# One level of Strassen's algorithm for the neighbour product A times g in a two-layer graph network kernel

## The reference

```python
h = jnp.maximum(_layernorm(x, axis=-1), 0.0)
x = x + _L0_gnn_ref(h, edge_weight, L0_gnn_bias, edge_index)     # h @ W.T + bias, W summed from the edges
h = jnp.maximum(_layernorm(x, axis=-1), 0.0)
x = x + _L1_gnn_ref(h, src, dst, W_self0, W_neigh0, b0, W_self1, W_neigh1, b1)
...
def _sage_layer(h, edge_src, edge_dst, deg_inv, W_self, W_neigh, b):
    agg = jax.ops.segment_sum(h[edge_src], edge_dst, num_segments=h.shape[0])
    return h @ W_self + (agg * deg_inv[:, None]) @ W_neigh + b
h = relu(_sage_layer(x, ..., W_self0, W_neigh0, b0)); out = _sage_layer(h, ..., W_self1, W_neigh1, b1)
```

## Time and profile before

| | before |
|---|---|
| time, median of 3 runs | 805.08 us (804.27 to 805.58) |
| span of the profiled execution | 802.3 us |
| time of the profiled execution outside its span | not shown; 2.8 us if it ran as the median |
| PE busy | 769.9 us (96%) |
| DVE busy | 485.3 us (60%) |
| ACT busy | 370.8 us (46%) |
| POOL busy | 412.3 us (51%) |
| DMA moved | 151.40 MB |

### The profile page before, as it was taken

The page is one execution under the profiler, slowest core; times in us unless marked ns, Lnnn a source line. Parts: engine busy times, 40 slices in busy tenths (PEclk is TensorE's granted clock), DMA queues, the critical chain, the costliest instruction groups (busy, mean ns, idle before and its releaser), DMA issues.

```text
span 802.3 us, 13275 instructions
## 1 busy us (share of the span) xinstructions
PE 769.9 (96%) x4553; PEld 639.1 (80%) x4554; DVE 485.3 (60%) x720; ACT 370.8 (46%) x526; POOL 412.3 (51%) x569
## 2 busy tenths in 40 slices
PE   3878999999999999999999999999999999999998
PEld 2767888888888888888887888888888888887787
DVE  7989377777554788867413342136568766246444
ACT  7757634333364232223246886453233223347653
POOL 5000167676649899765742210127899756724311
PEclk9689999999999999999999999999999999999999
DMA  3112456775565853577855654566745659667654
GB/s 111 42 57 92 137 178 192 237 228 186 191 225 193 275 169 116 182 230 269 278 180 189 210 158 105 171 209 229 261 134 164 202 198 332 216 206 268 223 163 142
DMA packets 83239, 151.40 MB, mean 189 GB/s; under 512 B 10979, under 2 KB 21278, under 8 KB 83168
## 3 DMA queue, kind: packets, MB, share of 16 engines
q1 hardware_dynamic: 61646, 102.65, 40.8%
q10 hardware_dynamic: 20002, 42.91, 15.0%
q0 software_dynamic: 1520, 4.92, 1.5%
HBM read 103.79 MB, written 46.65 MB: 188 GB/s over the span
## 4 chain that ended last, share of the span: by engine, by line
PE 82%; DVE 8%; DMA 3%; POOL 3%; issue 2%; ACT 2%; POOLq 0%; SPq 0%; ACTq 0%; DVEq 0%
PE bank L1449 45%; PE bank L1493 18%; PE bank L1384 13%; DVE L L1676 2%; DVE R L1661 2%; PE bank L1280 1%; PE bank L1296 1%; DVE L L1668 1%; PE bank L1510 1%; DMA cst<-prod1g_scratch 1%; DMA b<-in_L_gnn_b 1%; PE bank L1377 1%; PE bank L1275 1%; POOL split L935 1%; ACT Ax L1160 1%
## 5 line engine op out<-in xcount | busy, mean ns | idle before, releaser
L1449 PE MATMUL bank<-slot,split 128*128 128x512 f32 x1680 | 386.3, 390 | 0.2 <-POOL split L935 0.2
L1449 PEld LDWEIGHTS bank<-slot,split 128*128 128x128 f32 x1680 | 313.7, 188 | 66.0 <-issue 1.5
L897 POOL TENSOR_TENSOR AT<-AT,az 128x50 int32 (+3 forms) x288 | 95.5, 332 | 119.7 <-DMA az<-asum_scratch 78.7
L935 POOL TENSOR_TENSOR split<-stage,split 128x512 fp32r<-128x512 f32 x50 | 66.5, 1331 | 116.9 <-ACT split L1128 116.8
L1160 ACT CAST Ax<-AT 128x1280 fp32r<-128x1280 uint16 x40 | 106.6, 2667 | 34.5 <-PE bank L1493 27.5
L1811 DVE TENSOR_TENSOR slot<-T,slot 128x512 fp32r<-128x512 f32 x64 | 90.1, 1430 | 23.8 <-ACT slot L1119 22.0
L1384 PE MATMUL bank<-slot,split_m 128*128 128x512 f32 x320 | 91.2, 396 | 0.0
L1933 DVE SCALAR_TENSOR_TENSOR cst<-bank,dinv,stage 128x512 f32<-128x512 f32 (+1 forms) x41 | 30.3, 738 | 94.8 <-PE bank L1493 94.6
L1128 ACT CAST split<-stage 128x512 fp32r<-128x512 f32 x50 | 31.1, 624 | 118.1 <-PE bank L1449 67.4
L1493 PE MATMUL bank<-slot,Ax 128*128 128x512 f32 (+1 forms) x336 | 77.6, 383 | 0.4 <-ACT Ax L1160 0.4
L952 POOL TENSOR_TENSOR T<-T,wst 128x512 f32<-128x512 f32 x48 | 69.4, 1462 | 5.2 <-DMA wst<-in_L_gnn_W_self 5.2
(11 more groups left out here) (193 smaller groups left out, 1030.6 us busy)
## 6 DMA issues: line engine op xcount, KB each, us to landing
stage<-hT_scratch SPq DMA_DIRECT2D x90, 256.0 KB, 3.6
wst<-in_L_gnn_W_neigh SPq DMA_DIRECT2D x56, 256.0 KB, 4.3
wst<-in_L_gnn_W_self SPq DMA_DIRECT2D x56, 256.0 KB, 3.3
x1b_scratch<-x ACTq DMA_DIRECT2D x10, 512.0 KB, 6.1
hT_scratch<-hTs ACTq DMA_DIRECT2D x10, 512.0 KB, 3.2
stage<-prod0s_scratch SPq DMA_DIRECT2D x20, 256.0 KB, 3.0
hT_scratch<-h1s ACTq DMA_DIRECT2D x20, 256.0 KB, 3.5
stage<-prod1s_scratch SPq DMA_DIRECT2D x20, 256.0 KB, 2.7
```

The lines of the kernel that those rows point to most:

```text
L897: pool.tensor_tensor(a, a, az32[:, n % NZ, pairs * pos:pairs * (pos + 1)], ALU.add) \
L935: pool.tensor_tensor(split[:, v % 2, 1, :], source(v), split[:, v % 2, 0, :].bitcast(F32), ALU.subtract).then_inc(s_olo, 1)
L1449: last = pe.matmul(dense_bank(v, which)[:, :], split[:, v % 2, a, NT * k:NT * (k + 1)], slot[t % 2][:, b, HF * (HK * which + k):HF * (HK * ...
```

## The change

A times g is now also done with one level of Strassen's algorithm. A's rows and g's rows are halves of five tiles, g's columns halves of 512, so a layer has seven products of five row tiles, 35 steps u, each of 5 source tiles times 2 parts, 10 matmuls. The order of the steps is `A_SEQ`.

- **A turned once.** ACT copies the 16-bit counts of each of the ten row tiles from stride ten to contiguous (`turn`), at the product steps v = 10 to 19 of layer 0. Tile 0 goes to `az`, the others into `AT`.
- **Left operands.** Ring `Ax` of three, each 128x640. Where the quarter of A stands alone (p = 0, 1, 4) ACT widens it. Where it is a sum (p = 3, 2, 6, 5) DVE makes it (`left_sum`).
- **Right operands.** g12 and g21 are no longer stored to DRAM. DVE forms T1 and T2 (`first_sums`, at the last five product steps), T4 (`fourth_sum`) and T3 (`third_sum`); ACT rounds all seven (`right_hi`), POOL makes the rests (`right_lo`) except those of B21, which DVE makes (`b21_lo`).
- **Gathering.** ACT copies the first product out (`keep_first_A`); DVE adds products 3 and 2 (`take`), adds the kept sum times dinv into the sums tile (`sums_ready`), and takes the 20 outputs. Outputs come at u = 2, 4, 6, 8, 9, 17, 19, 21, 23 to 34. In layer 1 POOL adds x1 for 15 of the 20 tiles (`add_x1`), DVE for 5. Four sums tiles and four result tiles instead of two.
- **Bias.** It is added in `sub_products` at p = 0, p = 1 (once) and p = 2 instead of in `finish_tile`.
- **Stores.** Outputs of layer 1 are issued by ACT instead of POOL; the last tile is no longer split.
- **First weight blocks of layer 1.** ACT rounds them at u = 25 to 32, POOL instead of DVE makes the rest (`first_block_lo`).
- The heavier form is taken from a degree over 2048.

```diff
+A_SEQ = by_pairs(0, 1) + [(3, i) for i in range(PAIRS)] + by_pairs(2, 6) + by_pairs(5, 4)
+WIDENED = {0: (0, 0), 1: (0, 1), 4: (1, 1)}
+RIGHT_A = {0: "B11", 1: "B21", 2: "T1", 3: "T2", 4: "T4", 5: "T3", 6: "B22"}
...
+            def turn(n):
+                act.wait_ge(s_degs, n + 1)
+                ...
+                act.copy(turned(n).rearrange("p (s d) -> p s d", s=TN),
+                         ATd[:, NT * n:NT * (n + 1), :].rearrange("p d s -> p s d")).then_inc(s_turn, 1)
...
+            def neighbours(layer, u, heavy):
+                ...
+                wait_operand(pe, layer, u)
+                for k in range(PAIRS):
+                    if i == 0:
+                        wait_low(pe, layer, RIGHT_A[p], k)
+                    for b, part in enumerate(right(layer, RIGHT_A[p], k)):
+                        last = pe.matmul(sums, Ax[:, u % NR_A, NT * k:NT * (k + 1)], part, ...)
...
                 if p == 0:
+                    dve.tensor_tensor(q[:, 0, 1, i, :], dense_bank(v, 1)[:, :], b0[:, 0:HF], ALU.add).then_inc(s_evb, 1)
                     return
...
-                    elif p == 2:
-                        last = dve.tensor_tensor(second, first, ps, ALU.add)
+                    elif p == 2:
+                        link(dve.tensor_tensor(second, first, ps, ALU.add))
+                        last = dve.tensor_tensor(second, second, b0[:, HF:F], ALU.add)
...
+            def left_sum(layer, u):
+                dve.wait_ge(s_ag, VL * layer + u - NR_A + 1)
+                if p == 3:
+                    link(dve.tensor_tensor(s1[:, i, :], a21, a_block(1, 1, i), ALU.add))
+                    last = dve.tensor_tensor(to, s1[:, i, :], a11, ALU.subtract)
+                elif p == 2:
+                    last = dve.tensor_copy(to, s1[:, i, :])
+                elif p == 6:
+                    link(dve.tensor_tensor(s_pair[:, :], a11, a12, ALU.add))
+                    last = dve.tensor_tensor(to, s_pair[:, :], s1[:, i, :], ALU.subtract)
+                else:
+                    last = dve.tensor_tensor(to, a11, a21, ALU.subtract)
...
+            def products_of_A(layer, heavy):
+                b21_lo(layer, PAIRS - 1)
+                for u in range(VL):
+                    ...
+                    elif u + NR_A - 1 < VL and A_SEQ[u + NR_A - 1][0] not in WIDENED:
+                        left_sum(layer, u + NR_A - 1)
+                    if u in OUT_AT:
+                        sums_ready(layer, u)
+                    if 1 <= u <= PAIRS:
+                        fourth_sum(layer, u - 1)
+                    take(layer, u)
+                    if PAIRS - 1 <= u < 2 * PAIRS - 1:
+                        third_sum(layer, u - PAIRS + 1)
...
+                for k in range(PAIRS):                       # POOL, after the products
+                    right_lo(layer, "T2", k)
+                ...                                          # T1 2 to 4, B22, T3, then:
+                for k in range(PAIRS):
+                    if layer == 1 and k < PAIRS - 1:
+                        add_x1(PAIRS + k)
+                    right_lo(layer, "T4", k)
```

More of the change, by code:

```diff
@@ L819, in _ @@
+                if layer == 0:
+                    load_operand(VL)
+                    load_operand(VL + 1)
+                    load_bias(1)
+            for r in range(NO):
+                sp.wait_ge(s_out[r], 16 * (OL // NO))
         @block.gpsimd
```

757 lines of the change are left out of this document (502 added, 255 removed).

## The result

| | before | after |
|---|---|---|
| median of 16 runs each, us | 804.65 (802.88 to 806.31) | 802.19 (799.71 to 805.23) |
| span of the profiled execution, us | 802.3 | 798.8 |

The ratio is 0.9972, with a 95% interval of 0.996 to 0.9984: faster by 0.28%, 2.5 us. The forecast was 801.1. The totals agree; the terms agree less well, and the experiments are about those.

The account below looks back on a forecast made before the run. TensorE's queue was taken to bound the kernel, with VectorE setting layer 1's A times g after the change. Terms -7.9 + 1.2 + 0.5 + 2.2 = -4.0 us on 805.1 gave 801.1 us, range 786 to 814.

Parts of the forecast that it names:

- Layer 0's A times g: Layer 0's A times g: TensorE needs 88.6 us, uneven places add 4.0; 92.6 in all, 7.9 less than before.
- Layer 1's A times g: Layer 1's A times g: VectorE, slowed beside GpSimd, sets the stretch; 93.8 us, 1.2 us later than before.
- sign of being wrong: Layer 1's A times g: PE waits on DVE under 5 us, or DVE idles over 10 us while PE waits.
- the formula: A times g, layer 1: T = 66 us VectorE work + 64 exposed operations * 0.83 * 49/T, giving 93.8 us.
- The port time of 92.5 us: Layer 1's A times g, by the skill's whole-instruction exclusion: 49 + 64 * 0.68 us, against PE's 79.5; whole 799.8 us.
- The copy: Left sums in A times g: five VectorE copies a layer, between 0.48 and 0.82 us each, taken at 0.48, 2.4 together.
- The end: After the last A times g step: a take of 0.75 instead of 0.48 us and a whole-tile store, +0.5 us.
- Layer 0's products: Product steps at p = 2, layer 0: five exposed bias adds make GpSimd's operand late and VectorE later, +1.5 us.
- Layer 1's products: Product steps at p = 2, layer 1: the bias adds, with no degrees counted there, cost 0.7 us.
- rival 1: A times g: the cover holds, waits cost half, 0.37 us; layer 1 81.8, layer 0 90.1, whole 784.9 us; chance 0.3.
- rival 2: A times g: every exposed VectorE operation pays nearly a whole GpSimd operation, 1.0 us; whole 811.8 us; chance 0.2.
- the load loop: Layer 1's last twelve outputs: landing of 6 us makes it 9.6, not 9.1; 802.6 us; chance 0.05 with the heavier-form rival.

## Why the prediction was right, and where it was not

**Layer 0's A times g: right within its terms, and partly by luck.** 88.6 us for PE and 4.0 of stalls were predicted, 91.6 measured. The kernel without the rests, with no wait inside the stretch, gives some 89.0 for PE alone, so 2.6 are stalls. The waits named by the trace are 0.59 at u = 2 (1.5 predicted; the stretch starts 1.3 us late itself, which hides part) and 0.77 within u = 15 to 24 (2.5 predicted); another 0.43 near the start has no releaser. A wait costs somewhat more than its idle time, since the last matmul's recorded 0.39 us are longer than its spacing of 0.23. So PE was put 0.4 us too low and the stalls 1.4 too high.

**Layer 1's A times g: right in mechanism, 2 us too long.** DVE, not PE, sets it. Neither sign of being wrong showed: PE waits 9.1 us on DVE, where less than 5 would have refuted it, and DVE is idle for 2.1 us. VectorE's own work was put at 66 us; the rows of after, each at its duration alone, give 65.9. Waits were put at 64 * 0.83 * 49/93.8 = 27.8 us; the rows' sum, 94.5, less 65.9 gives 28.6. Here two errors nearly cancel, which is luck. GpSimd is at work 59.4 of 91.6 us, a share of 0.65, where 49/93.8 = 0.52 was put, since the lengthening of its own instructions was left out. The price beside a fully busy GpSimd is then 0.45/0.65 = 0.69 us, where 0.83 was put. What the formula lacked is that neighbouring instructions of DVE overlap in the records (752.45 plus 0.80, and the next at 753.17): 94.5 us of rows fill 89.5 us of time. Rows 0.7 us above the formula's 93.8, less 5.0 of overlap, with 2.3 in which DVE is not at work, come to the 91.8 of the stretch. As a rule for what an edit is worth the formula is weaker: with 2.4 us less of work (the copy) it gives 1.9 us less, and 0.7 came; with 13.5 less (the reading of PSUM) 10.1, and 4.6 came.

**The port time of 92.5 us.** The prediction worked it out from recorded lengths, as the sum of GpSimd's and VectorE's instructions. They do take turns, but a sum of recorded lengths counts the hidden start of each one twice: by the rows it is some 78 us, and the kernel without most of the PSUM reading ran in 87.2.

**The copy: base right, surroundings wrong.** It was taken at 0.48, the lower of two bounds. The prediction's rule gives a wait to operations with two SBUF inputs, and its list has 59 of these; its 64 is reached only with the five copies, for which it gives no reason. In the changed kernel this one line (least, median, most ns) took

```profile
L2185 DVE CAST Ax<-s x10: 485/978/1344, 455.5 to 759.0; 128x640 fp32r<-128x640 uint16 x10
```

and with GpSimd's rests gone

```profile
L2187 DVE CAST Ax<-s x10: 482/488/601, 456.6 to 752.5; 128x640 fp32r<-128x640 uint16 x10
```

So 0.48 is its time alone, and it does wait. The Trainium skill, VectorE: DVE Perf Modes, section The perf-mode tier table, gives an SBUF copy twice the rate of a two-input operation: 0.48 beside 0.83 for L2190, 1.7 times, agrees roughly. The section Who interferes with whom of SBUF — State Buffer counts copies at that rate among what contends with GpSimd, and the first of the two lines agrees.

**The end: +0.5 predicted, +0.9 measured.** The take lasts 0.75 as put, 0.27 more than before. The other 0.6 lies behind it, where ScalarE and not GpSimd now issues the store, of a whole tile; no run tells these two apart.

**Layer 0's products: the step that was mis-sized.** 1.5 us were put, 5.3 came, in three parts.
- *The bias addition, 2.5 us.* "In layer 0 DVE there idles 0.29 us ahead of a step's results" was read, and the delay then followed through GpSimd's operand alone (1.5 us). 1.23 us of the waits stand behind a reader of VectorE that comes after the addition in its queue, the degree count, and 0.58 behind GpSimd's operand. The prediction itself says that DVE's queue cannot reorder, and did not apply it here.
- *The branch, 1.1 to 1.6 us.* That much goes without it or with its order turned. That it could cost anything was in no step.
- *The bias load, 1.2 us.* It now stands early in SyncE's list, and the operand load behind it lands late. The prediction counts transfers under "DMA" and has no term for their order. This part is read from the traces and not from a run that changes it.

**Layer 1's products: right**, 0.8 against 0.7, and 1.0 goes with the bias.

That the total was within 1.1 us is luck: a term 3.8 us too small stood against three that were 1.0, 2.0 and 0.8 too cautious. The rivals: an operation's mean wait was 0.45 us, 28.6/64. The forecast comes to 0.43, 27.8/64, rival 1 to 0.25 and rival 2 to 0.54 by the same formula. The heavier form and the load loop did not come about; GpSimd waits for x1b loads (9.0 us ahead of eight additions) without anyone waiting for it, but for 0.5 us.

## What to carry to other kernels

An engine that by its own work would be a third idle (66 of 92 us) can fill up when work is moved to it beside a GpSimd that is two thirds busy. Price each VectorE instruction with two SBUF inputs, and fast copies, at its time alone plus the wait. Do not expect an edit to give back what it takes away. By their time alone, some 22 us of GpSimd's rests gave 0.44 us for each microsecond removed, 14 us of its additions 0.46, 13.5 us of left-hand sums 0.63, 13.5 us of PSUM reading 0.34, and the copy's move 0.30 (estimates from the rows, one trace each). The copy meets GpSimd too, so these do not sort neatly into work that meets it and work that does not. For an instruction added to an engine's queue, follow every reader behind it, small ones like a degree count too, and put it into the step that has none. Do the same for a load that is moved forward in an issuer's list: all the loads behind it wait with it.

## What was not expected of the hardware

- In nine kernels with the code of the form not taken ahead of the taken one PE stood 0.7 to 2.1 us in front of the taken form. In four with no branch or the taken form first it did not. Over the same work 1.1 to 1.6 us went. The kernel before, with its branch in the first order, has no such gap.
- A cast of 128x640 from 16 bits to fp32r is 0.48 us on VectorE alone and 0.79 to 1.34 beside a busy GpSimd, though it has one input.
- An instruction of VectorE with SBUF inputs and one of GpSimd took turns in all 66 of their meetings in layer 1's A times g: the later one ended its time alone less 0.12 to 0.19 us after the earlier one. The recorded length holds the wait, so 0.74 us shows as up to 1.82.
- GpSimd loses less to VectorE than VectorE to it: 38 of its instructions took 59.8 us in place of 48.6, 0.29 each, against 0.45 for each of VectorE's 64.
- A transfer that GpSimd issues costs it 0.85 to 1.17 us of its queue, and 20 of them made layer 1's products 8.3 us longer.
- After waits of 1.83 to 2.12 us of PE the granted clock fell to 0.50 for 3.4 us in the kernels without the rests and without most of the turning, twice each. After 2.02 us in layer 1 of the changed kernel, and 1.90 ahead of layer 0's A times g without the x1 additions, it did not.
